# Filler matmuls in the gaps of a recurrent layer: a 1024-step recurrence on one core

## The chip, the cores and the metric

The kernel runs on one core of one Trainium2 chip. The metric is the time of one execution on the device, in microseconds; lower is better. The time of a kernel is the median of its runs. A profile is one execution recorded by the hardware.

## What is computed

The model has four stages on an image of 32 x 32 positions, 32 channels and a batch of 2. Each stage has a mixing layer and a second layer. The one that matters here is the second layer of the third stage (L2), a recurrence over the 1024 positions taken as a sequence:

```python
def _L2_ffn_ref(x, W, V, gamma, beta):
    Wx = jnp.einsum('bti,hi->bth', x, W)
    flat = Wx.reshape(B * T, H)
    mean, var = jnp.mean(flat, axis=0), jnp.var(flat, axis=0)
    Wx = ((flat - mean) * rsqrt(var + 1e-05) * gamma + beta).reshape(B, T, H)
    def step(yt, wx_t):
        yt = sigmoid(wx_t + yt @ V.T)
        return (yt, yt)
    _, ys = jax.lax.scan(step, zeros((B, H)), swapaxes(Wx, 0, 1))
    return swapaxes(ys, 0, 1)
...
t = t + _L2_ffn_ref(_ln_t(t), ...)
x = x + window_attention(_ln_c(x))     # the mixing layer of the last stage
```

B = 2, T = 1024, H = 32. Each of the 1024 steps needs the one before.

## The kernel before

The image lies in SBUF as x, 64 partitions (batch and channel) by 1024 positions, in fp32. Each stage is a block: every engine has its own instruction stream in it, and the streams meet at its end. Between engines, semaphores order the work.

The function `recurrent` makes both recurrent layers. The first (L0, `swept`) guesses its states and sweeps over segments; the change doesn't touch that path. The second (L2) goes step by step.

Its setup is one block. It normalises x (class Norm: transposes to tokens on line 113, VectorE statistics, transposes back on line 120; the tokens lie in xn_tok, 128 partitions by 512). Then TensorE multiplies by W (line 734, four fp32 matmuls for the two batches, two instructions each), VectorE and ScalarE take the batch statistics and write the scaled result into partitions 32 to 63 of yx (lines 760 and 771). TensorE has no work after line 734. GpSimd zeroes yx (line 776).

The stage itself is a second block. In step t TensorE multiplies the columns of step t in yx, state in partitions 0 to 31 and input in 32 to 63, by v (line 791). It is an fp32 matmul with 64 rows of the array, 32 columns of weights and two moving columns; the trace has it as two LDWEIGHTS and two MATMUL instructions. ScalarE's sigmoid (line 801) writes the next state. Even and odd steps use different PSUM banks of p_z.

After step 512 half of the image is known. VectorE adds it to x (`add_half`), and the attention of the last stage begins on it beside the recurrence. TensorE's share is a Python generator, `Front.pe`: from step 517 on each step takes one turn of it, a turn being one small matmul (a piece) or nothing. Its pieces in order are transposes for the norm (lines 113 and 120, four each), q and k (line 1442, 16), v and the strided windows (lines 1452, 1460 and 1468, 8, 4 and 16) and 48 score matmuls (line 1360), with empty turns between groups where another engine needs time. These are 180 turns.
Of the kernel before, what the change touches and what calls it, by code (L numbers as in the profile page):

```python
# [6 lines left out]
BF16 = mybir.dt.bfloat16  # L7
# [6 lines left out]
NB, SIDE, C = 2, 32, 32  # L14
# [666 lines left out]
def more(nc, io, loc):  # L681
# [16 lines left out]
    def recurrent(tag, swept, use, beside):  # L698
# [5 lines left out]
        with ExitStack() as st:  # L704
# [5 lines left out]
            bn = sb(tag + "bn", [2 * C, NB, 2, 6], stack=st)  # L710
            mv = sb(tag + "mv", [2 * C, 8], stack=st)
            hi = slice(C, 2 * C)
            with ExitStack() as s2:
                p_a = ps(tag + "p_a", [128, T], stack=s2)
                p_b = ps(tag + "p_b", [R, T], stack=s2)
                p_w = ps(tag + "p_w", [2 * C, NB, T], stack=s2)
                norm = Norm(p_a, p_b, eps5)
                with nc.Block() as block:  # L718
                    @block.sync
                    def _(sp):  # L720
                        for t, src in ((w, io[tag + "_W"]), (v, io[tag + "_V"]), (gb, io[tag + "_gb"])):
                            sp.dma_start(t[:], src).then_inc(s("load"), 16)
                        beside.load(sp)
                        sp.wait_ge(*at("load", 48))

                    @block.tensor
                    def _(pe):
                        norm.pe(pe)
                        pe.wait_ge(*at("load", 48))
                        norm.wait_out(pe, 1)  # L730
                        for b in range(NB):
                            rows = slice(b * C, (b + 1) * C)
                            for h, c in halves():
                                last = pe.matmul(p_w[hi, b, c], w[rows], xn[rows, c], start=True, stop=True)
                            last.then_inc(s("wx"), 1)
                            if swept and b == 0:
                                beside.pe_sum(pe, p_a)
                        if swept:
                            beside.pe_square_sum(pe, p_a)

                    @block.vector
                    def _(dve):
                        link = chain(dve, "dve")
                        norm.dve(dve)
                        if swept:
                            beside.dve_spread(dve, link, p_a)

                        for b in range(NB):
                            dve.wait_ge(*at("wx", b + 1))
                            for h, c in halves():  # L750
                                link(dve.bn_stats(bn[hi, b, h], p_w[hi, b, c]))
                        dve.bn_aggr(mv[hi, 0:2], bn[hi].rearrange("p b h s -> p (b h s)")).then_inc(s("stats"), 1)
                        dve.wait_ge(*at("sd", 1))
                        dve.wait_ge(*at("load", 48))
                        link(dve.reciprocal(mv[hi, 5:6], mv[hi, 4:5]))
                        link(dve.tensor_tensor(mv[hi, 5:6], mv[hi, 5:6], gb[hi, 0:1], ALU.mult))
                        link(dve.tensor_tensor(mv[hi, 6:7], mv[hi, 5:6], mv[hi, 0:1], ALU.mult))
                        dve.tensor_tensor(mv[hi, 6:7], gb[hi, 1:2], mv[hi, 6:7], ALU.subtract).then_inc(s("shift"), 1)
                        dve.wait_ge(*at("shift", 1))
                        dve.tensor_scalar(by_batch[hi, 0:T, 1], p_w[hi, 1], mv[hi, 5:6], mv[hi, 6:7], ALU.mult, ALU.add)  # L760
                        unchain(link, "dve")

                    @block.scalar
                    def _(act):
                        norm.act(act)
                        act.wait_ge(*at("stats", 1))
                        act.activation(mv[hi, 4:5], mv[hi, 1:2], ACT.Sqrt, bias=eps5[hi, 0:1]).then_inc(s("sd"), 1)
                        if swept:
                            beside.act_root(act, p_a)
                        act.wait_ge(*at("shift", 1))  # L770
                        act.activation(by_batch[hi, 0:T, 0], p_w[hi, 0], ACT.Identity, bias=mv[hi, 6:7], scale=mv[hi, 5:6])

                    @block.gpsimd
                    def _(pool):

                        pool.memset(yx[0:C, 0:NB * T], 0.0)

            with ExitStack() as s2:
                p_z = ps(tag + "p_z", [128, 2, BANK], stack=s2)
                if not swept:  # L780

                    HALF, ROOTS = T // 2, T // 2 + 24
                    first = beside(s2)
                    with nc.Block() as block:
                        @block.tensor
                        def _(pe):
                            others = first.pe(pe)
                            for t in range(T):
                                if t:
                                    pe.wait_ge(s("state"), t)  # L790
                                pe.matmul(p_z[0:C, t % 2, 0:NB], v[:, 0:C], yx[:, NB * t:NB * (t + 1)], start=True, stop=True).then_inc(s("preact"), 1)  # L791
                                if t > HALF + 4:
                                    next(others, None)
                            for _ in others:
                                pass

                        @block.scalar
                        def _(act):
                            for t in range(T):
                                act.wait_ge(s("preact"), t + 1)  # L800
                                act.activation(yx[0:C, NB * (t + 1):NB * (t + 2)], p_z[0:C, t % 2, 0:NB], ACT.Sigmoid).then_inc(s("state"), 1)  # L801
                                if t == ROOTS:
                                    first.roots(act)

                        @block.vector
                        def _(dve):
                            dve.wait_ge(s("state"), HALF)
                            add_half(dve, by_batch, 0)
                            first.dve(dve)

                        @block.gpsimd
                        def _(pool):
                            first.pool(pool)
# [481 lines left out]
    with ExitStack() as st:  # L1295
# [100 lines left out]
        class Front:  # L1396
# [20 lines left out]
            def pe(self, pe):  # L1417
# [3 lines left out]
                pe.wait_ge(sig["half_added"], 3 * half + 3)  # L1421
                for j in range(4):
                    norm.turn(pe, half, j)
                    yield
                for _ in range(28):
                    yield
                for j in range(4):
                    norm.turn_back(pe, half, j)
                    yield
                for _ in range(20):  # L1430
                    yield
                pe.wait_ge(sig["load_at"], 16 * 12)
                made = 4 * half
                for g in (2, 0):
                    pe.wait_ge(sig[f"arranged{g}"], half + 1)
                    for m, wgt in enumerate((aq, ak)):
                        if made >= 2:
                            pe.wait_ge(sig["qk_read"], made - 1)
                        if half and g == 2:
                            pe.wait_ge(sig["at_max"], EARLY)  # L1440
                        for c in range(0, BANK, width):
                            ins = pe.matmul(p_q[:, m, c:c + width], wgt[:, WITHIN[g]], xo[:, g, half * BANK + c:half * BANK + c + width],
                                            start=True, stop=True)
                            if c + width == BANK:
                                ins.then_inc(sig["qk_made"], 1)
                            yield
                        made += 1
                        for _ in range(8):
                            yield
                for slot, g in enumerate((2, 0)):  # L1450
                    for t in range(4 * half, 4 * half + 4):
                        pe.matmul(p_e[:, slot, EC + t * JC:EC + (t + 1) * JC], xo[:, g, t * 128:(t + 1) * 128], av[:, slot], start=True, stop=True)
                        yield
                pe.wait_ge(sig["arranged3"], half + 1)
                cols = NB * 3 * HEADS * HC
                for f in range(2):
                    for w in range(2 * half, 2 * half + 2):
# [2 lines left out]
                        last = pe.matmul(p_e[:, 0, n * cols:(n + 1) * cols], xo[:, 3, start:start + 127 * W3 + 1:W3], ae3[:], start=True, stop=True)  # L1460
                        if (f, w) == (1, 2 * half + 1):
                            last.then_inc(sig["e_made"], 1)
                        yield
                pe.wait_ge(sig["arranged1"], half + 1)
                cols = 3 * HEADS * HC
                for w in range(8 * half, 8 * half + 8):
                    for b in range(NB):
                        last = pe.matmul(p_e[b * 64:(b + 1) * 64, 1, w * cols:(w + 1) * cols], xo[:, 1, w:w + 63 * W1 + 1:W1], ae1[:, b], start=True, stop=True)
                        if (w, b) == (8 * half + 7, 1):
                            last.then_inc(sig["e_made"], 1)  # L1470
                        yield
                if half == 0:
                    pe.wait_ge(sig["qk_read"], 4)
                    for u in range(EARLY):
                        if u >= 2:
                            pe.wait_ge(sig["at_max"], u - 1)
                        for n in range(BANK // width):
                            e, part = divmod(n, BANK // width // len(units[u][2]))
                            ins = score(pe, p_q[:, u % 2], u, e, units[u][2][e], part, width)
                            if n == BANK // width - 1:  # L1480
                                ins.then_inc(sig["at_scores"], 1)
                            yield

            def roots(self, act):
                self.norm.act_roots(act, self.half)
# [475 lines left out]
```

## Time and profile before

| | us |
|---|---|
| median of 3 runs | 1204.1 |
| lowest, highest | 1201.9, 1204.3 |
| the profiled execution | 1202.4 |
| its span in the trace | 1200.6 |
| mean granted clock of TensorE over the span | 0.66 |

The span runs from the first to the last instruction; the execution's own time has 1.8 us around it. On the page, PE is a matmul and PEld a load of weights on TensorE, DVE is VectorE, ACT ScalarE, POOL GpSimd. "Busy" adds up the durations of an engine's instructions, "idle before" the gaps ahead of them, with the instruction whose semaphore ended the gap.

### The profile page before, as it was taken

The numbers are of one execution on the slowest core, as the hardware profiler recorded it, in microseconds if no ns is written. First come the engines' busy times: TensorE is split into PE (matmuls) and PEld (weight loads), VectorE is DVE, ScalarE is ACT, GpSimd is POOL, SyncE is SP. The second block draws the span as 40 slices with busy tenths as digits, with TensorE's granted clock in tenths as the row PEclk, the third lists the DMA queues.
The fourth block names the chain that finished last, engine by engine and source line by source line (L and its number), as shares of the span: only waits on it lengthen the run. The fifth ranks groups of instructions, "written<-read, shape, count | busy, mean of one in ns | idle before, by whom it ended". The sixth has DMA issues, their size and how long they took to land. (4 is left out here: it accounts for less than half of the span.)

```text
span 1200.6 us, 11335 instructions
## 1 busy us (share of the span) xinstructions
PE 747.2 (62%) x4114; PEld 435.2 (36%) x4114; DVE 479.7 (40%) x828; ACT 454.9 (38%) x1547; POOL 226.0 (19%) x130
## 2 busy tenths in 40 slices
PE   4807777777767655545555555557995555548975
PEld 1302222232233323223333333335773333325753
DVE  5597999999855534500000000012020000018652
ACT  3446556565424422033333333332212333335531
POOL 2276666666600000020000000000000000002200
PEclk9956999999995575555555555555555555555995
DMA  2020000000000000100000000000000000000000
GB/s 61 1 53 1 0 1 0 1 0 1 0 5 1 1 20 9 58 1 1 1 1 1 1 0 1 1 1 1 1 1 1 1 1 1 1 1 1 1 20 10
DMA packets 9570, 7.68 MB, mean 6 GB/s; under 512 B 7154, under 2 KB 8066, under 8 KB 9224
## 3 DMA queue, kind: packets, MB, share of 16 engines
q1 hardware_dynamic: 9512, 6.93, 2.4%
q8 instruction: 33, 0.54, 0.2%
q14 instruction: 25, 0.20, 0.1%
HBM read 5.09 MB, written 0.26 MB: 4 GB/s over the span
## 5 line engine op out<-in xcount | busy, mean ns | idle before, releaser
L791 PE MATMUL L2p_z<-L2yx,L2v 64*32 64x2 f32 x2048 | 267.9, 199 | 242.1 <-ACT L2yx L801 236.3
L801 ACT ACTIVATE L2yx<-L2p_z 32x2 f32<-32x2 f32 x1024 | 165.2, 161 | 389.2 <-PE L2p_z L791 389.2
L791 PEld LDWEIGHTS L2p_z<-L2yx,L2v 64*32 64x32 f32 x2048 | 180.4, 135 | 340.0 <-ACT L2yx L801 316.0
L692 DVE COPY xn<-L2yx 32x512 f32<-32x512 f32 x2 | 0.8, 417 | 431.1 <-ACT L2yx L801 264.2
L573 POOL TENSOR_TENSOR hc<-hs,cb 128x1024 f32<-128x1024 f32 x64 | 150.9, 2358 | 81.6 <-DVE hs L560 81.6
L560 DVE TENSOR_TENSOR_SCAN hs<-d_a,p_bb 128x1024 f32<-128x1024 f32 x64 | 146.3, 2286 | 8.9 <-ACT d_a L539 0.7
L526 PE MATMUL p_y<-hc,ident 128*128 128x512 f32 x256 | 122.5, 602 | 3.4 <-POOL hc L573 3.0
L1498 POOL COPY xo<-xn 64x256 f32<-64x256 f32 (+1 forms) x6 | 3.9, 691 | 555.9 <-DVE xn L157 555.9
L539 ACT ACTIVATE d_a<-step,decay 128x1016 f32<-128x1016 f32 x64 | 73.1, 1142 | 86.9 <-DVE hs L560 86.4
L510 PE MATMUL p_bb<-b_parts,pick 96*128 96x512 bf16 x128 | 40.5, 399 | 81.9 <-DVE hs L560 49.2
L555 DVE TENSOR_TENSOR p_bb<-drive,p_bb 128x1024 f32<-128x1024 f32 x64 | 77.3, 1207 | 6.2 <-PE p_bb L510 6.2
L543 ACT ACTIVATE cb<-p_cb 128x1024 f32<-128x1024 f32 x64 | 65.5, 1024 | 3.2 <-PE p_cb L516 3.1
L526 PEld LDWEIGHTS p_y<-hc,ident 128*128 128x128 f32 x256 | 48.7, 192 | 47.0 <-issue 31.6
L510 PEld LDWEIGHTS p_bb<-b_parts,pick 96*128 96x128 bf16 x128 | 7.8, 99 | 134.8 <-DVE hs L560 99.0
L516 PE MATMUL p_cb<-c_parts,pick 96*128 96x512 bf16 x128 | 39.9, 395 | 1.2 <-ACT cb L543 1.2
L1360 PE MATMUL atp_q<-kk,q 128*128 128x128 f32 x96 | 38.2, 502 | 0.0
L869 PE MATMUL L0p_z<-L0yx,L0v 64*32 64x64 f32 x192 | 30.2, 306 | 9.9 <-PEq L718 4.3
L1382 ACT ACTIVATE scored<-scored,anmx 128x256 f32<-128x256 f32 (+1 forms) x64 | 28.3, 442 | 17.2 <-DVE anmx L1375 17.1
L1626 PE MATMUL atp_o<-apt,vv 128*32 128x128 f32 x192 | 26.0, 282 | 2.3 <-ACT apt L1722 2.3
L869 PEld LDWEIGHTS L0p_z<-L0yx,L0v 64*32 64x32 f32 x192 | 17.6, 141 | 22.2 <-ACT L0yx L889 16.4
L889 ACT ACTIVATE L0yx<-L0p_z 32x64 f32<-32x64 f32 x96 | 20.1, 215 | 13.4 <-PE L0p_z L869 13.1
L1360 PEld LDWEIGHTS atp_q<-kk,q 128*128 128x128 f32 x96 | 24.0, 310 | 0.8
(387 smaller groups left out, 854.5 us busy)
## 6 DMA issues: line engine op xcount, KB each, us to landing
y_seq<-in_pick SPq DMA_DIRECT2D x1, 768.0 KB
b_parts<-part SPq DMA_DIRECT2D x3, 256.0 KB, 3.6
c_parts<-part SPq DMA_DIRECT2D x3, 256.0 KB, 4.4
pos<-in_pos SPq DMA_DIRECT2D x1, 512.0 KB, 3.6
ao<-in_at_o SPq DMA_DIRECT2D x1, 512.0 KB, 4.4
L1w<-in_L_w SPq DMA_DIRECT2D x1, 297.0 KB
L3w<-in_L_w SPq DMA_DIRECT2D x1, 297.0 KB
x_tok<-in_x SPq DMA_DIRECT2D x2, 128.0 KB, 2.8
```

The source lines that it names most:

```text
L510: last = pe.matmul(p_bb[:, u % 2, h * BANK:(h + 1) * BANK], pick[:, n], b_parts[:, k, c], start=True, stop=True)
L516: last = pe.matmul(p_cb[:, h * BANK:(h + 1) * BANK], pick[:, n], c_parts[:, k, c], start=True, stop=True)
L526: last = pe.matmul(p_y[:, c], ident[:], hc[:, v % RING, c], start=(n == 0), stop=(n == NS - 1))
L539: act.activation(dst[:, :, 1:L], src[:, :, 1:L], ACT.Exp, scale=decay[:, k, n:n + 1]).then_inc(sig["d_a"], 1)
L543: act.activation(cb[:, u % RING], p_cb[:], ACT.Copy).then_inc(sig["c_copied"], 1)
L555: dve.tensor_tensor(p_bb[:, u % 2], drive[:, k, c0:c0 + UC], p_bb[:, u % 2], ALU.mult).then_inc(sig["d_bu"], 1)
L560: dve.tensor_tensor_scan(hs[:, u % RING], d_a[:, u % 2], p_bb[:, u % 2], 0.0, ALU.mult, ALU.add).then_inc(sig["scanned"], 1)
L573: pool.tensor_tensor(hc[:, u % RING], hs[:, u % RING], cb[:, u % RING], ALU.mult).then_inc(sig["hc"], 1)
L791: pe.matmul(p_z[0:C, t % 2, 0:NB], v[:, 0:C], yx[:, NB * t:NB * (t + 1)], start=True, stop=True).then_inc(s("preact"), 1)
L801: act.activation(yx[0:C, NB * (t + 1):NB * (t + 2)], p_z[0:C, t % 2, 0:NB], ACT.Sigmoid).then_inc(s("state"), 1)
L869: pe.matmul(p_z[0:C, f, 0:NB * n], v[:, 0:C], by_batch[:, cols], start=True, stop=True).then_inc(s("preact"), 1)
L1360: return pe.matmul(dst[:, c:c + width], q[:, WITHIN[g], j, t * 128:(t + 1) * 128], kk[:, WITHIN[g], k0:k0 + width], start=True, stop=True)
```

## The change

In the setup block of L2, GpSimd copies the normalised tokens xn_tok into a new bf16 tile `filler` (128 partitions by 512) when they are ready. TensorE waits for that and, after line 734, runs 16 matmuls on it, 128 rows, 128 columns of weights, 512 moving columns, into a PSUM bank that nobody reads any more.

In the stage, `fill(n)` runs n matmuls on partitions 64 to 127 of `filler` (array rows 64 to 127, 128 weight columns, 512 moving columns, bf16) into the second bank of p_z; nobody reads them. Step 0 has five, every later step two, except the steps that take a piece of attention, which have none. The step's own results now share the first bank of p_z. The generator gets more empty turns: one after each piece of lines 1442 to 1468 and two after each score piece. It yields True after a piece and False for an empty turn.

```diff
+            if not swept:
+                filler = sb(tag + "filler", [128, BANK], BF16, stack=st)
...
                         if swept:
                             beside.pe_square_sum(pe, p_a)
+                        else:
+                            pe.wait_ge(s("filler"), 1)
+                            for _ in range(16):
+                                pe.matmul(p_a[:, 0:BANK], filler[:, 0:128], filler[:], start=True, stop=True)
...
                         pool.memset(yx[0:C, 0:NB * T], 0.0)
+                        if not swept:
+                            norm.wait_tokens(pool)
+                            pool.tensor_copy(filler[:], xn_tok[:].rearrange("p j r -> p (j r)")).then_inc(s("filler"), 1)
...
+                    p_step = p_z[0:C, 0].rearrange("p (h n) -> p h n", h=2)
+                    away = slice(2 * C, 128)
...
+                            def fill(n):
+                                for _ in range(n):
+                                    pe.matmul(p_z[:, 1], filler[away, 0:128], filler[away], start=True, stop=True)
+
                             for t in range(T):
                                 if t:
                                     pe.wait_ge(s("state"), t)
-                                pe.matmul(p_z[0:C, t % 2, 0:NB], v[:, 0:C], yx[:, NB * t:NB * (t + 1)], start=True, stop=True).then_inc(s("preact"), 1)
-                                if t > HALF + 4:
-                                    next(others, None)
+                                pe.matmul(p_step[:, t % 2, 0:NB], v[:, 0:C], yx[:, NB * t:NB * (t + 1)], start=True, stop=True).then_inc(s("preact"), 1)
+                                if t == 0:
+                                    fill(5)
+                                elif t <= HALF + 4:
+                                    fill(2)
+                                elif next(others, False) is not True:
+                                    fill(2)
...
                 for j in range(4):
                     norm.turn(pe, half, j)
-                    yield
+                    yield True
                 for _ in range(28):
-                    yield
+                    yield False
...
                             if c + width == BANK:
                                 ins.then_inc(sig["qk_made"], 1)
-                            yield
+                            yield True
+                            yield False
...
                             if n == BANK // width - 1:
                                 ins.then_inc(sig["at_scores"], 1)
-                            yield
+                            yield True
+                            yield False
+                            yield False
```

## Rows read from the trace of the kernel before

**Rows 1.** The page: busy time of the engines, and the costliest group of instructions.
```profile
PE 747.2 (62%) x4114; PEld 435.2 (36%) x4114; DVE 479.7 (40%) x828; ACT 454.9 (38%) x1547; POOL 226.0 (19%) x130
...
L791 PE MATMUL L2p_z<-L2yx,L2v 64*32 64x2 f32 x2048 | 267.9, 199 | 242.1 <-ACT L2yx L801 236.3
```

**Rows 2.** Instructions of line 801: ns min/median/max, first and last start in us.
```profile
L801 ACT ACTIVATE L2yx<-L2p_z x1024: 161/161/163, 514.9 to 1072.1; 32x2 f32<-32x2 f32 x171
```

**Rows 3.** The timeline around one bare step: start us, duration us, instruction.
```profile
778.56 0.26 PE L791 MATMUL L2p_z<-L2yx,L2v 64*32 64x2 f32 x2 [0.25 <-ACT L2yx L801]
...
778.86 0.16 ACT L801 ACTIVATE L2yx<-L2p_z 32x2 f32<-32x2 f32 x1 [0.35 <-PE L2p_z L791]
...
779.07 0.26 PE L791 MATMUL L2p_z<-L2yx,L2v 64*32 64x2 f32 x2 [0.25 <-ACT L2yx L801]
```

**Rows 4.** The timeline around the square root of step 536.
```profile
790.33 1.28 ACT L161 ACT_TABLE_LOAD   x1
...
793.46 0.27 PE L791 MATMUL L2p_z<-L2yx,L2v 64*32 64x2 f32 x2 [2.83 <-ACT L2yx L801]
```

**Rows 5.** The timeline around one step with a score matmul.
```profile
871.27 0.27 PE L791 MATMUL L2p_z<-L2yx,L2v 64*32 64x2 f32 x2
...
871.47 0.80 PE L1360 MATMUL atp_q<-kk,q 128*128 128x128 f32 x2
...
872.19 0.27 PE L791 MATMUL L2p_z<-L2yx,L2v 64*32 64x2 f32 x2
```

**Rows 6.** Busy time by stretch (PE, PEld, DVE, ACT, POOL), then granted clock, DMA.
```profile
880.00:900.00 20.00, 20.00 (x89) 14.70 (x89) 5.05 (x33) 3.40 (x22) 0.00 (x0) 0.50 0.00 0
```

**Rows 7.** Instructions of lines 113 (layer L2, layer L0) and 1157.
```profile
L113 PE MATMUL L2p_a<-ident,x x8: 311/311/335, 496.8 to 497.5; 64*128 64x64 f32 x8
...
L113 PE MATMUL L0p_a<-ident,x x8: 221/222/243, 354.4 to 354.9; 64*128 64x64 f32 x8
...
L1157 PE MATMUL L1p_b<-L1hid,L1w x32: 192/193/212, 465.9 to 467.6; 128*32 128x2 f32 x32
```

**Rows 8.** The timeline of bf16 matmuls, at clock 0.50 (94 us) and 1.00 (111 us).
```profile
94.68 1.01 PE L510 MATMUL p_bb<-b_parts,pick 96*128 96x512 bf16 x2 [32.55 <-PEq L399]
95.49 1.06 PE L516 MATMUL p_cb<-c_parts,pick 96*128 96x512 bf16 x2
...
111.25 0.60 PE L510 MATMUL p_bb<-b_parts,pick 96*128 96x512 bf16 x2
111.69 0.59 PE L516 MATMUL p_cb<-c_parts,pick 96*128 96x512 bf16 x2
```

**Rows 9.** The timeline of matmuls on parts of the array's rows.
```profile
361.76 3.59 PE L734 MATMUL L0p_w<-xn,L0w 32*32 32x512 f32 x4 [0.76 <-ACT xn L170]
...
504.10 3.63 PE L734 MATMUL L2p_w<-xn,L2w 32*32 32x512 f32 x8 [0.76 <-ACT xn L170]
...
347.71 2.78 PE L614 MATMUL p_tr<-ident,y_tok 64*64 64x64 f32 x48
```

**Rows 10.** The timeline at the end of the setup.
```profile
511.98 1.34 DVE L760 TENSOR_SCALAR L2yx<-L2p_w,L2mv 32x1024 f32<-32x1024 f32 x1
```

**Rows 11.** Stretches around the start of line 1053's dense matmuls (from 429.77).
```profile
429.50:433.00 3.50, 3.23 (x4) 0.97 (x5) 0.00 (x0) 0.13 (x1) 0.00 (x0) 0.50 0.00 0
433.00:435.00 2.00, 2.00 (x6) 0.68 (x5) 0.00 (x0) 0.00 (x0) 0.00 (x0) 1.00 0.00 0
```

**Rows 12.** A stretch with pauses, and one of dense matmuls on 64 rows.
```profile
324.00:334.00 10.00, 5.31 (x21) 2.69 (x21) 4.38 (x4) 0.20 (x1) 3.81 (x2) 1.00 0.01 2
480.70:487.50 6.80, 6.80 (x8) 1.75 (x9) 3.39 (x5) 0.00 (x0) 0.00 (x0) 0.50 0.00 0
```

**Rows 13.** Stretches in which TensorE pauses.
```profile
62.00:64.00 2.00, 0.13 (x1) 0.00 (x0) 1.89 (x4) 1.82 (x2) 1.15 (x1) 1.00 0.00 0
64.00:65.00 1.00, 0.00 (x0) 0.00 (x0) 1.00 (x3) 0.99 (x3) 0.14 (x1) 0.68 1.32 262
...
1141.00:1143.00 2.00, 0.23 (x2) 0.00 (x0) 1.90 (x10) 0.51 (x3) 0.00 (x0) 1.00 0.00 0
```

More of the change, by code:

```diff
@@ L800, in _ @@
                                 act.wait_ge(s("preact"), t + 1)
-                                act.activation(yx[0:C, NB * (t + 1):NB * (t + 2)], p_z[0:C, t % 2, 0:NB], ACT.Sigmoid).then_inc(s("state"), 1)
+                                act.activation(yx[0:C, NB * (t + 1):NB * (t + 2)], p_step[:, t % 2, 0:NB], ACT.Sigmoid).then_inc(s("state"), 1)
                                 if t == ROOTS:
@@ L1445, in pe @@
                                 ins.then_inc(sig["qk_made"], 1)
-                            yield
+                            yield True
+                            yield False
                         made += 1
                         for _ in range(8):
-                            yield
+                            yield False
                 for slot, g in enumerate((2, 0)):
@@ L1452, in pe @@
                         pe.matmul(p_e[:, slot, EC + t * JC:EC + (t + 1) * JC], xo[:, g, t * 128:(t + 1) * 128], av[:, slot], start=True, stop=True)
-                        yield
+                        yield True
+                        yield False
                 pe.wait_ge(sig["arranged3"], half + 1)
@@ L1462, in pe @@
                             last.then_inc(sig["e_made"], 1)
-                        yield
+                        yield True
+                        yield False
                 pe.wait_ge(sig["arranged1"], half + 1)
@@ L1470, in pe @@
                             last.then_inc(sig["e_made"], 1)
-                        yield
+                        yield True
+                        yield False
                 if half == 0:
@@ L1481, in pe @@
                                 ins.then_inc(sig["at_scores"], 1)
-                            yield
+                            yield True
+                            yield False
+                            yield False
             def roots(self, act):
```

## The prediction

> **What bounds the kernel now.** I read the page first [rows 1]. TensorE is busy 62% of 1200.6 us, so no engine is the bound; chains are. The costliest line is the matmul of 791, and it waits for the sigmoid of line 801. The list of that sigmoid gives the stage: 1024 of them from 514.9 to 1072.1 us, 557 us or 46% of the span, every one 161 ns [rows 2]. The timeline shows one step: the two instructions of the fp32 matmul take 0.26 us, 0.04 later the sigmoid runs 0.16, 0.05 later the next matmul starts: 0.514 us from matmul to matmul [rows 3]. 1024 steps at 0.514 are 526 us; the other 31 us lie in the second half. One step lasts 3.09 us, 2.6 more than the others (TensorE waits 2.83 before 793.46): ScalarE loads its tables twice, 1.28 us each, around the root of line 161 [rows 4]. And each step with an attention piece on TensorE is longer: with a score matmul (line 1360) 0.92 us from 871.27 to 872.19 [rows 5], 48 of them, and I count 16 of line 1442 the same. 64 x 0.4 = 26; what is left of the 31, some 3, belongs to the 36 small pieces (lines 113, 120, 1452 to 1468). Last, the stretches by clock: the whole stage runs at a granted clock of 0.50, 1.2 GHz, also where score matmuls fill TensorE [rows 6].
>
> **What the change is worth if its clock holds.** It can shorten only TensorE's 0.26 us of a step and the pieces; sigmoid, semaphores and table loads stay. No such pair at 2.4 GHz is in the trace. Near it: the transposes of line 113 take 311 ns each at clock 0.50 and 222 at 1.00; line 1157, two columns wide like ours, takes 193 at 0.50, and its 32 start some 54 ns apart (465.9 to 467.6) [rows 7]. Of the 222, 53 are the 64 columns, twice for fp32, at 2.4 GHz, which leaves 169 for a narrow one. So the pair goes from 54 + 207 to about 27 + 172 = 0.20 us, and a step from 0.514 to 0.46. The bounds are 0 and half of 0.26, 0.13 a step; line 113 is the nearest row, so I keep 0.054. 1024 x 0.054 = 55 us.
>
> The pieces: a pair of line 1360 starts 0.20 after the step's matmul and 0.72 before the next one [rows 5]. The 0.72 is weights and columns, which halve with the clock; 0.36 and 0.1 to 0.2 are 0.46 to 0.56, little over a bare step. I put a step with such a piece at 0.58, excess 0.12 for 0.40, in 64 steps: 18 us; the small ones give 2. Together 20 (bounds 8 and 27). Spreading costs nothing by itself: the generator of pieces goes from 180 turns to 320 and starts at step 517, so it ends at 837 of 1024. Each wait in it has empty turns ahead of it, as before, and these shrink only with the step: the 28 ahead of line 120 from 14.4 to 12.9 us.
>
> **The fillers' own time.** A bf16 matmul of 512 columns is in the trace: at clock 0.50 the pairs of lines 510 and 516 start 0.81 us apart, and 512 columns at 1.2 GHz are 0.427 each; at 1.00 the pairs start 0.44 apart, 0.22 each [rows 8]. Two fillers are thus 0.44 us in a fast step of 0.46 and fit, barely. In a slow one they are 0.85, over the 0.514 that a step lasts now.
>
> **Do they hold up the steps?** Fillers use array rows 64 to 127, the step's matmul 0 to 63. The trace has two cases of different rows at once. Line 734 in layer L0, four instructions of one row group, takes 3.59 us; in layer L2 two row groups with the same output partitions, eight instructions, take 3.63: they run two at a time, though the second group stands behind the first in program order. And the 64x64 transposes of line 614, with the row half changing from one to the next, come 48 in 2.78 us, 58 ns each at mostly half clock, where 64 fp32 columns alone are 107 [rows 9]. I take nothing for the collision; bounds 0 and what the rival below gives. The Trainium skill ("TensorE: Matmul & The Clock Gate", the section on packing small matmuls) has matmuls start and end in strict program order. By it a step's matmul couldn't end before the fillers ahead of it, some 0.70 us after the step before began, and with 0.25 from there to the next start, two steps would be 0.95 and the total near 1144. Line 734 speaks against it.
>
> **The setup.** TensorE is free from 507.7 us, and the setup ends about 513.4 with the writes to L2yx [rows 10]. 16 fillers of 128 rows are 6.8 us at 0.43 and less once the clock rises. It rose 3.2 us into the dense matmuls of line 1053 [rows 11]. So 8 run slow and 8 at 0.22, 5.2 us, end 512.9, under the cover; if all run slow they end at 514.5. Cost 0 to 1.2 us; I take 0.5. GpSimd's added copy has its tokens at 501.9 and 5.8 us before TensorE asks; its cover is line 734's matmuls. The five fillers of step 0 (1.1 us) lie under a 1.28 us table load like those of [rows 4].
>
> Sum against the profiled run, 1202.4 us (span 1200.6, 1.8 around it): 1202.4 - 55 - 20 + 0.5 = 1128. The median of the runs is 1204.1, 1.7 above: **1129 us**.
>
> **Does the clock hold?** For: from 324 to 334 us it stayed at 1.00 while TensorE was busy 5.3 of 10 us [rows 12]; the fillers work nearly all the time, on half of the rows. Against: dense 64-row matmuls (lines 1246 and 1247) ran without a gap from 480.7 to 487.5 and the clock stayed at 0.50 [rows 12]. So once lost it will hardly come back, and a filler then costs double. What fillers on 64 rows do for a clock that is already high no row shows.
>
> **Rival 1, slower: the clock falls in the stall of step 537.** ScalarE's table loads leave TensorE 3.09 us with two fillers, so 2.6 us idle. The clock fell some 2.2 us after the last matmul, which ended at 62.13 (a mean of 0.68 from 64 to 65 is a fall at 64.36); the pause from 1141.2 to 1143 it survived [rows 13]. 2.6 is longer than both, but what went before differs. From there each step lasts at least its two slow fillers: 486 x 0.854 = 415, some 4 more for long pieces, where the trace has 1072.6 - 793.5 = 279 [rows 2, 4]. +140, less 29 gained in 537 steps x 0.054: **1314**. It decides as soon as the clock falls before about step 850 (0.34 lost per slow step against 0.054 gained).
>
> **Rival 2: fillers and steps exclude each other.** The step's matmul is 64 x 32, the filler 64 x 128; both cases above have one shape, and no row has two. Then a step is fillers 0.44, a weight load 0.05 and the overhead of a piece step now (0.92 less 0.85 of weights and columns, 0.07): 0.57, +57 us less 15 from pieces: **1245** with the clock held; with it lost in the stall 1.03 a step: +30 + 221 = **1454**. The Trainium skill ("TensorEngine Tiling (Array Packing)", key properties) says that a change of tiling mode drains TensorE, which is this case. No row here decides it.
>
> **Rival 3: the clock falls at once**, because half of the rows isn't enough to keep it: 1020 x 0.854 = 871 for 557, **1516**. The setup's dense run then only delays it.
>
> **How the numbers follow.** Forecast 0.57, own range 1105 to 1160 (bounds of step and pieces). Rival 1 0.22: its pause is long by [rows 13], but fillers stand right before and after it. Rival 2 0.12, of it 0.04 at 1245. Rival 3 0.06. 0.03 is left for a clock that comes and goes near the time of before. The range must take in rival 1 to hold 8 in 10: 1105 to 1330. A measurement of this kernel tells about 0.2% from no change. Faster 0.59, same 0.02, slower 0.39.
>
> **What the profile after would show.** Right: granted clock 1.00 from about 513 us past 1000, steps 0.46 us apart, sigmoids still 161 ns with line 791's pair at 0.20, steps with a score matmul under 0.6, stage 480 us. Rival 1: the clock falls within 3 us of the second table load pair, then 0.85 a step. Rival 2: 0.57 or more with the clock at 1.00, and no filler over a step's matmul. Rival 3: 0.85 from the start. Wrong altogether I would be if the pair of line 791 takes 0.26 us at full clock too, or if fillers lengthen the sigmoid's read of the bank beside them.

## The result and the profile after

| | before | after |
|---|---|---|
| median, us | 1204.19 (4 runs) | 1791.97 (4 runs) |
| lowest, highest | 1201.89, 1205.02 | 1791.18, 1792.63 |
| span of the profiled execution | 1200.6 | 1790.8 |
| mean granted clock | 0.66 | 0.608 |
| stage, first to last sigmoid | 557.2 | 1143.4 |

The ratio is 1.4885, 95% interval 1.486 to 1.4911: slower by half, and far outside the range of 1105 to 1330. In the changed file the step's matmul is line 807 (it was 791), the filler 802, the sigmoid 821 (801), the setup's dense run 745 and the score matmul 1380 (1360).

First the page: busy time of the engines, TensorE's clock in 40 slices, the two groups of the recurrence. They answer to [rows 1].

```profile
PE 1579.4 (88%) x5981; PEld 554.9 (31%) x5981; DVE 479.9 (27%) x828; ACT 454.9 (25%) x1547; POOL 226.9 (13%) x131
...
PEclk9779999956555555555555555555555555555596
...
L802 PE MATMUL L2p_z<-L2filler 64*128 64x512 bf16 x1851 | 949.2, 615 | 0.0
...
L807 PE MATMUL L2p_z<-L2yx,L2v 64*32 64x2 f32 x2048 | 267.6, 198 | 1.6 <-ACT L2yx L821 1.2
```

TensorE is now busy in nearly the whole stage, the work of the other engines is what it was, and the clock row reads 5 from the stage's start to its end. Ahead of the step's matmul the engine was idle for 242.1 us and now is for 1.6: that matmul stands behind fillers instead. The list of the sigmoid gives the stage; each is still 161 ns [rows 2].

```profile
L821 ACT ACTIVATE L2yx<-L2p_z x1024: 161/161/163, 516.7 to 1660.1; 32x2 f32<-32x2 f32 x171
```

Now busy time by stretch (us and count of PE, PEld, DVE, ACT, POOL), then granted clock, DMA share, GB/s:

```profile
509.40:513.60 4.20, 4.20 (x11) 1.45 (x11) 3.56 (x9) 0.29 (x1) 0.00 (x0) 0.50 0.10 34
513.70:520.40 6.70, 6.31 (x36) 2.30 (x34) 1.33 (x1) 3.52 (x8) 5.04 (x1) 1.00 0.01 2
520.60:560.00 39.40, 39.40 (x137) 10.24 (x136) 0.00 (x0) 5.60 (x35) 3.44 (x2) 0.50 0.00 0
```

The setup's dense run does raise the clock, at 513.7, and 6.8 us later it is gone, with fillers running all the time. It doesn't return in the stage. The timeline (start us, duration us, instruction) shows one step at full clock, one at half, and one with a score matmul, which answer to [rows 3] and [rows 5]:

```profile
517.56 0.22 PE L807 MATMUL L2p_z<-L2yx,L2v 64*32 64x2 f32 x2
...
517.71 0.60 PE L802 MATMUL L2p_z<-L2filler 64*128 64x512 bf16 x2
517.82 0.16 ACT L821 ACTIVATE L2yx<-L2p_z 32x2 f32<-32x2 f32 x1 [0.52 <-PE L2p_z L807]
...
518.24 0.22 PE L807 MATMUL L2p_z<-L2yx,L2v 64*32 64x2 f32 x2
```
```profile
700.16 0.26 PE L807 MATMUL L2p_z<-L2yx,L2v 64*32 64x2 f32 x2
...
700.36 1.03 PE L802 MATMUL L2p_z<-L2filler 64*128 64x512 bf16 x2
700.46 0.16 ACT L821 ACTIVATE L2yx<-L2p_z 32x2 f32<-32x2 f32 x1 [0.99 <-PE L2p_z L807]
...
701.32 0.26 PE L807 MATMUL L2p_z<-L2yx,L2v 64*32 64x2 f32 x2
```
```profile
1300.06 0.26 PE L807 MATMUL L2p_z<-L2yx,L2v 64*32 64x2 f32 x2
...
1300.25 0.80 PE L1380 MATMUL atp_q<-kk,q 128*128 128x128 f32 x2
...
1300.98 0.27 PE L807 MATMUL L2p_z<-L2yx,L2v 64*32 64x2 f32 x2
```

At half clock a step is 1.16 us long (0.514 before). The sigmoid ends at 700.62 and its result waits 0.7 us, because the next matmul starts only when both fillers have gone through. In parts: 0.19 us from the step's matmul to the first filler, two fillers at 0.427, 0.11 from the end of the second's columns to the next matmul: 1.154. At full clock it is 0.15 + 0.43 + 0.10 = 0.68, longer than the old step at half clock. A step with a score matmul takes 0.92, as before.

This accounts for the time. 1851 fillers, less the five of step 0, are 923 steps with two. 923 x (1.154 - 0.514) = 591; some six of them ran at full clock (-3), and the stall of step 537, in which TensorE waits for ScalarE's two table loads, swallows its fillers (its step is 2.45 us, 3.09 before, -1). That is 587; the stage grew by 586. Another 4 us of the span lie outside the stage, 1.8 ahead of its first sigmoid and 2.2 behind its last. In the twelve runs below, which all have this setup, the first sigmoid starts anywhere from 514.7 to 517.0 and the part behind the last lasts 127.7 to 130.5 (130.7 here, 128.5 before), and nofill is as fast as the kernel before; so I take them for such spread, which I followed no further.

The setup, in the timeline, against [rows 10]: the dense run ends at 515.10, VectorE's last write at 515.03.

```profile
509.37 5.73 PE L745 MATMUL L2p_a<-L2filler 128*128 128x512 bf16 x16
...
513.69 1.34 DVE L766 TENSOR_SCALAR L2yx<-L2p_w,L2mv 32x1024 f32<-32x1024 f32 x1
```

So two things happened together, the second and the third rival of the prediction: fillers and steps exclude each other (one runs only when the other is through), and the clock falls almost at once. The questions for the chip were whether the exclusion comes from the shapes, what the fall of the clock hangs on, and what is left of the idea. The fillers' output is read by nobody, so a run that changes them computes the same.

### The profile page after: what moved, and what is told of

Same layout as the page of the kernel before. It is cut to its first block and busy times, and to the rows that moved or that the text cites. A ratio compares the mean times of both kernels' runs of the same rounds, so it can differ in the third digit from the quotient of the medians.

```text
span 1790.8 us, 15070 instructions
## 1 busy us (share of the span) xinstructions
PE 1579.4 (88%) x5981; PEld 554.9 (31%) x5981; DVE 479.9 (27%) x828; ACT 454.9 (25%) x1547; POOL 226.9 (13%) x131
## 5 line engine op out<-in xcount | busy, mean ns | idle before, releaser
L802 PE MATMUL L2p_z<-L2filler 64*128 64x512 bf16 x1851 | 949.2, 615 | 0.0
L807 PEld LDWEIGHTS L2p_z<-L2yx,L2v 64*32 64x32 f32 x2048 | 180.2, 135 | 789.3 <-ACT L2yx L821 772.1
L802 PEld LDWEIGHTS L2p_z<-L2filler 64*128 64x128 bf16 x1851 | 115.7, 104 | 14.8
L543 ACT ACTIVATE cb<-p_cb 128x1024 f32<-128x1024 f32 x64 | 65.5, 1024 | 4.1 <-PE p_cb L516 4.0
L1391 DVE CUSTOM_DVE_ANT_0 scored<-atp_q,pos 128x256 f32<-128x256 f32 (+1 forms) x32 | 9.9, 355 | 142.0 <-PE atp_q L1380 142.0
```

The source lines that it names most:

```text
L543: act.activation(cb[:, u % RING], p_cb[:], ACT.Copy).then_inc(sig["c_copied"], 1)
L802: pe.matmul(p_z[:, 1], filler[away, 0:128], filler[away], start=True, stop=True)
L807: pe.matmul(p_step[:, t % 2, 0:NB], v[:, 0:C], yx[:, NB * t:NB * (t + 1)], start=True, stop=True).then_inc(s("preact"), 1)
```

## The experiments

### One filler, two shapes

The kernel one64 is the change with one filler a step instead of two:

```diff
 elif t <= HALF + 4:
-    fill(2)
+    fill(1)
 elif next(others, False) is not True:
-    fill(2)
+    fill(1)
```

> The change with one filler a step in place of two (64 rows, 128 weight columns, as in the change). Theory E (filler and step exclude each other: a step is 0.19 from its matmul to the first filler, 0.427 for each slow filler and 0.11 from the end of the last to the next matmul, 1.154 us with two): 0.73 us a step at clock 0.50, total about 1400. Theory C (they run beside each other and only the fillers' own backlog of 0.85 us made the step long): the step is bare again at 0.514 at clock 0.50 and the total near 1200. If the clock holds at 1.00 because the work is less broken up: 0.47 a step, about 1150; I expect it to fall within 10 us of the stage's start.

Measured: 1400.37 us, one run, beside 1204.86 for the kernel before. Its timeline:

```profile
700.36 0.26 PE L807 MATMUL L2p_z<-L2yx,L2v 64*32 64x2 f32 x2
...
700.56 0.60 PE L802 MATMUL L2p_z<-L2filler 64*128 64x512 bf16 x1
...
701.09 0.26 PE L807 MATMUL L2p_z<-L2yx,L2v 64*32 64x2 f32 x2
```

One slow filler is 0.427 us and would fit into a step of 0.514 if it ran beside it. The step is 0.727: 0.19 + 0.427 + 0.11. 923 x 0.213 = 197, and 1204 + 197 = 1401, the time that was measured.

The kernel one64x32 is one64 with the filler cut to the width of the step's matmul, 32 columns of weights, on the same rows, into the same bank:

```diff
-pe.matmul(p_z[:, 1], filler[away, 0:128], filler[away], start=True, stop=True)
+pe.matmul(p_z[0:C, 1], filler[away, 0:C], filler[away], start=True, stop=True)
```

> As one64, but the filler loads only 32 weight columns and writes 32 partitions, so it has the same shape (64 x 32) as the step's matmul and lies on other rows. Theory D (the change of shape between 64 x 128 and 64 x 32 is what makes TensorE finish one before the other): the fillers run beside the steps, 0.514 us a step at clock 0.50, total near 1200. Theory S (a matmul that waits for a semaphore, or comes behind another in program order, starts only after the ones ahead of it are through, whatever the shape): 0.73 a step as in one64, total near 1400.

Measured: 1203.48 us (one run; before 1204.86). Timeline, and stretches by clock:

```profile
699.98 0.12 PEld L807 LDWEIGHTS L2p_z<-L2yx,L2v 64*32 64x32 f32 x1 [0.34 <-ACT L2yx L821]
...
699.99 0.60 PE L802 MATMUL L2p_z<-L2filler 64*32 64x512 bf16 x1
...
700.49 0.12 PEld L807 LDWEIGHTS L2p_z<-L2yx,L2v 64*32 64x32 f32 x1 [0.34 <-ACT L2yx L821]
```
```profile
511.70:518.40 6.70, 5.59 (x38) 1.95 (x36) 1.49 (x2) 3.85 (x10) 4.90 (x1) 1.00 0.00 0
518.50:560.00 41.50, 41.50 (x245) 14.27 (x243) 0.00 (x0) 13.05 (x81) 3.67 (x2) 0.50 0.00 1
```

The filler starts 0.01 us after the step, not 0.19, and the step takes 0.51 as without any filler. The same 928 fillers of 512 columns cost 197 us in one shape and nothing in the other. The Trainium skill ("TensorEngine Tiling (Array Packing)", Key Properties) has a change of tiling mode drain TensorE, where tiles of one mode run in parallel; these two traces agree with it, and price it at half clock: the next step waits for the whole filler, and for 0.11 us behind it. The clock fell in both kernels, 6.8 us after it had risen.

### Shape or width?

That a narrow filler runs beside a narrow step could also mean that only narrow matmuls can. same128 is one64 with the step's matmul widened to the filler's shape, all 128 columns of v, of whose results the sigmoid still reads the first 32 partitions:

```diff
-p_step = p_z[0:C, 0].rearrange("p (h n) -> p h n", h=2)
+p_step = p_z[:, 0].rearrange("p (h n) -> p h n", h=2)
...
-pe.matmul(p_step[:, t % 2, 0:NB], v[:, 0:C], ...)
+pe.matmul(p_step[:, t % 2, 0:NB], v[:], ...)
```

> One filler a step as in one64 (64 rows, 128 weight columns), but the step's matmul also has 128 weight columns (v is zero beyond column 32), so both have the shape 64 x 128. The step's own loads of weights grow, so a bare step is longer. Theory D (only different shapes exclude each other): the filler runs beside it, the step is its own chain, near 0.6 us. Theory W (a filler of 128 columns covers the step's columns 0 to 31 and that is what excludes): one after the other, 0.8 us a step or more.

Measured: 1522.68 us (one run; before 1204.58 in this group of runs). Timeline:

```profile
699.72 0.37 PE L807 MATMUL L2p_z<-L2yx,L2v 64*128 64x2 f32 x1 [0.22 <-ACT L2yx L821]
...
699.73 0.60 PE L802 MATMUL L2p_z<-L2filler 64*128 64x512 bf16 x1
...
699.95 0.35 PE L807 MATMUL L2p_z<-L2yx,L2v 64*128 64x2 f32 x1
700.34 0.16 ACT L821 ACTIVATE L2yx<-L2p_z 32x2 f32<-32x2 f32 x1 [0.67 <-PE L2p_z L807]
700.55 0.28 PEld L807 LDWEIGHTS L2p_z<-L2yx,L2v 64*128 64x128 f32 x1 [0.34 <-ACT L2yx L821]
```

And a step of the same run that takes a score matmul, so that no filler stands beside it:

```profile
1101.38 0.50 PEld L807 LDWEIGHTS L2p_z<-L2yx,L2v 64*128 64x128 f32 x2 [0.34 <-ACT L2yx L821]
1101.38 0.58 PE L807 MATMUL L2p_z<-L2yx,L2v 64*128 64x2 f32 x2 [0.22 <-ACT L2yx L821]
...
1102.00 0.16 ACT L821 ACTIVATE L2yx<-L2p_z 32x2 f32<-32x2 f32 x1 [0.67 <-PE L2p_z L807]
```

By time alone this run speaks for the rival: 0.83 us a step. The lines say otherwise. The filler starts at 699.73, between the two instructions of the step's own matmul; the next step starts 0.05 after the sigmoid, held up by no filler. What became long is the step's own path: its sigmoid starts 0.62 us after the matmul, where it was 0.30 in the kernel before, since each of the two fp32 instructions now loads 128 columns of weights (0.28 and 0.33 us, together 0.50, where the two narrow loads were 0.18). The filler has no part in it: without one beside it the sigmoid starts 0.62 us after the matmul too (1101.38 to 1102.00). My expectation had that term too small. So equal shape decides, not a small width. The Trainium skill ("TensorE: Matmul & The Clock Gate", Part 3) has matmuls start and end in strict program order. This trace agrees only if the two instructions of an fp32 matmul count as one: the filler, which stands behind the step's matmul in the program, starts 0.22 us ahead of that matmul's second instruction. Whether they also end out of order no run here shows.

### What holds the clock

dense64 leaves the steps without fillers but gives step 0 a run of 64, in the original shape:

```diff
 if t == 0:
-    fill(5)
-elif t <= HALF + 4:
-    fill(2)
-elif next(others, False) is not True:
-    fill(2)
+    fill(64)
+elif t > HALF + 4:
+    next(others, None)
```

> The setup's dense run as in the change; then step 0 has 64 fillers of 64 rows without a break and the steps have none. Theory H (64 rows hold a high clock as long as they are dense, and the fall at 520 us came because the step's gaps thinned them): all 64 start 0.216 apart (13.8 us), the clock falls a few us after them, and the first bare steps after them show the bare step at 1.00, near 0.47 us. Theory L (64 rows don't hold it at any density): the clock falls within 7 us, the rest of the 64 start 0.427 apart. Total in both about 1215 to 1225: some 14 to 25 us for the 64 fillers, the rest as before.

Measured: 1215.94 us (one run; before 1204.86). Stretches, and the timeline of a step behind the run:

```profile
515.70:529.60 13.90, 13.90 (x66) 5.93 (x66) 0.00 (x0) 1.20 (x2) 8.43 (x2) 1.00 0.01 1
531.40:600.00 68.60, 35.14 (x268) 23.63 (x268) 0.00 (x0) 21.44 (x134) 0.00 (x0) 0.50 0.00 1
```
```profile
530.00 0.22 PE L807 MATMUL L2p_z<-L2yx,L2v 64*32 64x2 f32 x2 [0.25 <-ACT L2yx L819]
...
530.47 0.22 PE L807 MATMUL L2p_z<-L2yx,L2v 64*32 64x2 f32 x2 [0.25 <-ACT L2yx L819]
```

64 fillers on half of the rows, back to back, keep the clock at 1.00 for their 14 us; it falls at 531.3, behind four bare steps. So work on 64 rows alone can go with a clock that stays up. This run also measures the disputed 0.46: a bare step at full clock takes 0.471 us, 0.043 less than at half clock.

two64x32 is the change itself, two fillers and all, with only the shape of one64x32:

> The change with nothing altered but the shape of its fillers in the steps: 32 weight columns instead of 128, so they have the shape of the step's matmul. Two a step, as in the change. They no longer hold up a step, so TensorE is busy on 64 rows for 0.43 of each 0.47 us. Theory H (dense work on 64 rows holds a high clock; in the change the exclusion thinned it): clock 1.00 and 0.47 us a step through the first half, then a fall near the four pieces of line 113 or the stall, and 0.85 a step or a little more from there; total 1300 to 1350. Theory L2 (fillers of 32 columns hold nothing, whatever their density): the clock falls within 10 us and each step lasts its two slow fillers, 0.85 us; total near 1530.

Measured: 1311.22 us (one run; before 1204.58).

```profile
513.50:762.50 249.00, 248.30 (x2104) 71.65 (x2102) 3.98 (x9) 86.38 (x527) 8.68 (x2) 1.00 0.00 1
763.00:900.00 137.00, 135.35 (x679) 60.82 (x677) 10.59 (x20) 30.46 (x174) 1.98 (x3) 0.50 0.00 1
```
```profile
600.01 0.19 PE L807 MATMUL L2p_z<-L2yx,L2v 64*32 64x2 f32 x1
...
600.02 0.39 PE L802 MATMUL L2p_z<-L2filler 64*32 64x512 bf16 x1
...
600.48 0.19 PE L807 MATMUL L2p_z<-L2yx,L2v 64*32 64x2 f32 x1
```

Only the shape differs from the change, and the clock stays up for 249 us, with steps of 0.47 us that have two fillers beside them. It was lost with one filler in the same 0.47 us (one64x32, at 518.45) and with two in 0.684 (the change, at 520.50). In both shapes, then, the clock stayed up where fillers on 64 rows followed each other with little or no pause (dense64, two64x32) and fell where they had longer pauses; in the change it is the exclusion that makes the pauses. The clock falls at 762.6, 2 us behind the first four steps with pieces, which have no filler; from there a step is at least its two slow fillers, 0.854. That is the course of the first rival, but the fall came at step 524 and not in the stall of step 537. That its total, 1314, was within 3 us is partly luck: an earlier fall (13 steps at 0.38, some 5 us) and a gain of 0.043 a step for 0.054 (some 6 us) would have made it 1325.

two128 is the change with its two fillers on all 128 rows, which gives them up as neighbours of the step but keeps their rhythm:

```diff
-pe.matmul(p_z[:, 1], filler[away, 0:128], filler[away], start=True, stop=True)
+pe.matmul(p_z[:, 1], filler[:, 0:128], filler[:], start=True, stop=True)
```

> The change with its two fillers a step on all 128 rows in place of rows 64 to 127; nothing else differs. This separates the two losses: the exclusion stays, the clock should stay high. Theory: clock 1.00 and 0.684 us a step (0.15 + 0.43 + 0.105, as the change had in its first 4 us at 1.00), through most of the stage, with a fall possible at the stall (two fillers in 3 us) or among the pieces; if it falls at the stall the rest runs at 1.154. Total 1370 with the clock held throughout, about 1590 with a fall at the stall. Rival (the exclusion shrinks with 128 rows, or the clock falls at once as in the change): 1204 or 1792.

Measured: 1462.64 us (one run; before 1203.55).

```profile
513.50:870.00 356.50, 356.41 (x2073) 128.43 (x2073) 1.78 (x3) 84.56 (x518) 8.62 (x2) 1.00 0.00 1
1000.00:1200.00 200.00, 200.00 (x769) 81.26 (x768) 12.97 (x80) 30.94 (x192) 0.00 (x0) 0.50 0.00 1
1222.00:1330.00 108.00, 108.00 (x631) 38.90 (x630) 0.00 (x0) 25.30 (x157) 0.00 (x0) 1.00 0.00 1
```

The steps are those of the change, 0.69 at full clock (600.24 to 600.93) and 1.16 at half (1099.96 to 1101.12). But the clock holds for 360 us where the change's held for 7, until 873.6, again 2 us behind the four transposes of line 113. It comes back three times while the steps go on: at 876.7 until the stall (886.9), from 972.1 to 989.2, and at 1221.2, 34 us behind the last score matmul (1187.1); the change's never did. The steps have the same rhythm in both kernels, and only the rows of the fillers differ: so the rows mattered here, beside the pauses. It also says what each cause is worth in the change: of its 588 us, 329 go when the rows are doubled (1792 to 1463), 481 when the shape is made equal (1792 to 1311). The two add up to more than 588, since each makes the other dearer.

### A filler on all rows that fits

one128 takes one 128-row filler a step, twelve in the stall (t == ROOTS + 1), and none in steps with a piece (its fillers have the shape of two128):

```diff
+elif t == ROOTS + 1:
+    next(others, None)
+    fill(12)
 elif t <= HALF + 4:
-    fill(2)
+    fill(1)
 elif next(others, False) is not True:
-    fill(2)
+    fill(1)
```

> One filler a step, on all 128 rows, and 12 in the step of the stall; the rest of the change stays. Since filler and step exclude each other anyway, the rows cost nothing. Theory E with a clock that follows the rows in use: clock 1.00 through the stage, a step of 0.15 + 0.216 + 0.105 = 0.47 us, stage 490 us, total about 1145. If the clock falls all the same: 0.73 a step, total about 1400.

Measured: 1270.49 us (2 runs), ratio 1.0544 (1.0514 to 1.0575).

```profile
518.00 0.22 PE L807 MATMUL L2p_z<-L2yx,L2v 64*32 64x2 f32 x2
...
518.15 0.39 PE L802 MATMUL L2p_z<-L2filler 128*128 128x512 bf16 x1
...
518.47 0.22 PE L807 MATMUL L2p_z<-L2yx,L2v 64*32 64x2 f32 x2
```
```profile
513.50:762.00 248.50, 240.41 (x1544) 120.70 (x1571) 3.02 (x4) 86.36 (x523) 8.68 (x2) 1.00 0.00 1
763.00:776.00 13.00, 12.78 (x50) 4.94 (x51) 1.68 (x5) 4.94 (x18) 0.00 (x0) 0.50 0.00 0
```

At full clock such a filler excludes the step too, and costs nothing: 0.15 + 0.216 + 0.10 is 0.47, just what the step lasts anyway. The clock fell at 762.5, after four steps with a transpose of line 113 and no filler (760.40 to 762.1). The twelve fillers in the stall raised it again at 776.2; it fell at 786.4, 2 us behind the next four pieces without a filler (line 120), and the slow steps with a filler, 0.733 each, made the loss.

always128 is the same with a filler in the steps with pieces too:

> As one128, but a step with an attention piece has its filler too, so that no step is without dense work on 128 rows. Theory: the clock fell in one128 at 762.5 us because four steps with pieces of line 113 in a row had no filler. Then it holds here past those, past the stall (12 fillers) and past the pieces: 0.471 us a step, pieces some 0.1 to 0.3 longer than that, total 1155 to 1175. Rival: it falls at the stall or among the pieces of line 1442 all the same, 0.73 a step from there, total 1250 to 1280.

Measured: 1288.53 us (4 runs), ratio 1.0676 (1.0628 to 1.0724). The clock still fell at 763.3, in the same four transposes, whose steps were 0.675 long with the filler; after the stall it held from 780.4 to 841.8, six times as long as in one128, past the transposes of line 120, and fell again among the small pieces, before the first score matmul (884.0). So the missing fillers weren't the whole reason, and what in the steps with pieces brings the clock down stays open. Fillers at half clock are the price of trying.

### The parts without fillers, and what is left of the idea

nofill keeps the setup's dense run and the wider spread of the pieces, and no filler in the steps:

```diff
-if t == 0:
-    fill(5)
-elif t <= HALF + 4:
-    fill(2)
-elif next(others, False) is not True:
-    fill(2)
+if t > HALF + 4:
+    next(others, None)
```

> The change without its fillers in the steps: the setup's dense run and the wider spread of the attention pieces are left. Theory: the dense run is hidden behind VectorE's statistics, a few steps at the start run at 0.47, the spread costs nothing, and the time is that of the kernel before, 1202 to 1206. Rival: the wider spread or the setup costs something of its own, 1210 or more.

Measured: 1204.47 us (8 runs, before 1204.58), ratio 0.9997 (0.9987 to 1.0007). Both cost nothing. The clock was up for 3.4 us, from 512.7.

half128 uses fillers only where they pay: one of 128 rows in steps 1 to 516, ahead of the first piece, and from there on the kernel before:

```diff
+if t <= HALF + 4:
+    fill(1 if t else 5)
+else:
+    next(others, None)
```

> One filler a step on 128 rows for steps 0 to 516 only, five in step 0; from 517 on the kernel is as before (its turns not spread, no fillers). Theory: 516 steps at 0.471 instead of 0.514, 22 us less, then the clock falls and nothing else changes: 1180 to 1184. Rival: the setup or a late fall gives part of it back, 1188 or more.

Measured: 1181.73 us (4 runs), ratio 0.9817 (0.98 to 0.9833). half64x32 is the same with two narrow fillers a step beside the step's matmul, `fill(2 if t else 5)`:

> As half128, but with two fillers a step of rows 64 to 127 and 32 weight columns, the shape that ran beside the steps in two64x32. Theory: the same 0.471 us a step, so the same time as half128 within 2 us, 1180 to 1184. Rival: a filler still at work when a step is ready delays it somewhat, 1186 or more.

Measured: 1179.73 us (4 runs), ratio 0.9807 (0.979 to 0.9823). Beside the step or in its gap makes no difference beyond these 2 us, as long as the filler fits. 516 x 0.043 = 22 us is what a full clock is worth on bare steps, and 21.8 and 23.8 were measured.

burst128 adds a second stretch: ahead of the first score piece 17 fillers at once, then one in each step without a piece, and a score piece every second step:

```diff
+if t <= HALF + 4:
+    fill(1 if t else 5)
+    hot = False
+else:
+    turn = next(others, False)
+    if turn == "burst":
+        hot = True
+        fill(17)
+    elif hot and turn is not True:
+        fill(1)
```

> As half128, and before the first score matmul a burst of 17 dense fillers on 128 rows (7 us at clock 0.50, less once it rises), after which every step without a piece has one filler and scores take every second step. Theory: the clock rises in the burst and stays to the end: some 375 steps at 0.471 for 0.514 (16 us), 48 score steps at about 0.6 for 0.92 (15 us), less 6 for the burst: 25 us under half128, 1155 to 1160. Rival: score steps are too thin and the clock falls again among them, 0.73 a step from there: 1210 or more.

Measured: 1156.1 us (4 runs), ratio 0.9606 (0.959 to 0.9622), the fastest here, 47 us ahead of the kernel before. The score matmul is line 1384 in it.

```profile
844.20:1028.00 183.80, 182.66 (x1177) 96.20 (x1175) 12.79 (x78) 61.24 (x375) 0.00 (x0) 1.00 0.00 1
```
```profile
860.16 0.22 PE L807 MATMUL L2p_z<-L2yx,L2v 64*32 64x2 f32 x2
...
860.31 0.49 PE L1384 MATMUL atp_q<-kk,q 128*128 128x128 f32 x2
...
860.73 0.22 PE L807 MATMUL L2p_z<-L2yx,L2v 64*32 64x2 f32 x2
```

The burst made one step 6.1 us long (839.47 to 845.60), 5.6 more than before it, and bought 184 us at full clock: score steps at 0.57 us instead of 0.92, and bare ones at 0.47.

## Why the prediction was wrong

- **The fillers beside the steps: the step that failed.** "I take nothing for the collision" leant on [rows 9], where matmuls of different rows overlap. Both cases there have one shape on both row groups; filler and step have two. The prediction said so itself, under the second rival, and still gave that rival 0.12. The runs showed an exclusion by shape (one64 against one64x32, and same128). It cost 0.21 us a step at full clock, in some six steps, and 0.64 at half, in the other 917 of 923.
- **The size in that rival** was also short: 0.57 and 1.03 us against 0.684 and 1.154. It summed fillers, a weight load and an overhead, but not that the first filler itself waits 0.15 to 0.19 for the step's matmul.
- **The clock: failed.** I took it to hold, with [rows 12] as the case for it, which shows a pause survived by matmuls of all rows and nothing of 64. It fell 6.8 us after the rise. The third rival had this, at 0.06, and its 1516 lacked the exclusion. Its reason, that half of the rows isn't enough, was half right: dense64 and two64x32 held the clock with 64 rows, and two128 held it with 128 in the rhythm in which the change lost it.
- **The cases were not alternatives.** I priced either exclusion or a clock lost at once, and exclusion thins out the fillers, so it makes that loss likely. Both together, from the prediction's own terms, are about 1204 + 923 x (1.03 - 0.514) = 1680, and with the measured step 1795. No case of mine went over 1516, and the range ended at 1330.
- **A bare step at full clock: right, a little large.** Forecast 0.46, measured 0.471 (dense64, half128). The pair is 0.22 us, not 0.20; the gain 0.043, not 0.054, so 1024 steps would give 44 us and not 55.
- **A step with a score matmul at full clock: right.** Forecast 0.58, measured 0.57 in burst128. From the piece to the next step it is 0.42 us, not half of 0.72; what the forecast put on top covered the difference.
- **The fillers' own time: right**, 0.427 and 0.22 us as in [rows 8].
- **Setup and spread: right.** The dense run ends 0.07 us behind VectorE, and nofill is at 0.9997. The clock rose 4.3 us into that run (3.2 in [rows 11]), so it took 5.73 us and not 5.2.
- **Where the clock is in danger: partly right.** With a filler that fits, it fell right behind the first pieces (762.5 to 763.4), 13 to 16 steps ahead of the stall that I named; those pieces I had not thought of as a danger. In two128 it was up again when the stall came and fell in it (886.9).

## What to carry to other kernels

Before putting work on spare rows of the array, compare its tile shape with that of the work beside it: here one 64x32 filler beside the 64x32 step was free, and at half clock one 64x128 filler beside it cost 0.21 us a step, two 0.64. When two risks of a change feed each other, price them together, and let the range reach that sum. A filler pays only where it fits into the gap at the clock it gets; where the clock is going to be low, leave it out, as burst128 does.

## What was unexpected in the hardware

A filler on 64 rows of another shape costs a step as much as one on all 128 rows, the step's own among them: 0.727 (one64) against 0.733 us (one128) at half clock.

Dense fp32 matmuls on 64 rows did not raise the clock in 6.8 us [rows 12], but 64 fillers on 64 rows held it for 14 us, and two fillers a step for 249. Two 128-row fillers a step went with a rise from half clock (two128, at 876.7, 972.1 and 1221.2), two 64-row ones with none in 1139 us.

Full clock is worth little to this chain of narrow fp32 matmuls: 0.043 us of 0.514, since only the pair moves with it, from 0.26 to 0.22 us, and the sigmoid starts 0.26 us after the matmul instead of 0.30.
